# More load buffers, later kept loads and one re-cut row visit in a two-layer graph kernel

## What is computed

```python
def _L0_gnn_ref(X, adj, W, b):
    adj_hat = adj + eye
    d_inv_sqrt = 1.0 / sqrt(sum(adj_hat, axis=1))
    adj_norm = adj_hat * d_inv_sqrt[:, None] * d_inv_sqrt[None, :]
    return relu(adj_norm @ (X @ W) + b)

def _L1_gnn_ref(x, adj, weight, self_weight):
    support = x @ weight
    output = relu(support + adj @ support + x @ self_weight)
    return pair_norm(output)          # one mean per feature and one norm over all rows

x = _layernorm(x + _L0_gnn_ref(x, adj, L0_gnn_W, L0_gnn_b))
x = _layernorm(x + _L1_gnn_ref(x, adj, L1_gnn_weight, L1_gnn_self_weight))
```

## Time and profile before

| | before |
|---|---|
| median of 3 runs | 2022.59 us (2019.74 to 2023.22) |
| the profiled execution | 2021.88 us, its span 2020.1 us |
| stage 0 | 0 to 94.5 us |
| stages 1 to 7 | 94.5, 259.2, 406.4, 529.0, 630.3, 711.3, 772.0 (starts) |
| phase 2 | 852.1 to 1516.0 |
| phase 3 | 1516.0 to 1962.5 |
| tail | 1962.5 to 2020.1 |
| busy: PE, DVE, ACT | 1767.3, 1517.5, 1241.7 us |
| mean granted TensorE clock | 0.958 of full speed |

### The profile page before, as it was taken

The page is one execution under the profiler, slowest core; times in us unless marked ns, Lnnn a source line. Parts: engine busy times, 40 slices in busy tenths (PEclk is TensorE's granted clock), DMA queues, the critical chain, the costliest instruction groups (busy, mean ns, idle before and its releaser), DMA issues.

```text
span 2020.1 us, 21098 instructions
## 1 busy us (share of the span) xinstructions
PE 1767.3 (87%) x7682; PEld 1408.9 (70%) x7682; DVE 1517.5 (75%) x2165; ACT 1241.7 (61%) x1821; POOL 21.5 (1%) x34
## 2 busy tenths in 40 slices
PE   1199989889898986887999999999998999999992
PEld 0176777666776765665777887878886878778872
DVE  4586686686777785797775757557558999999996
ACT  3467667577666552563554445444446888888875
POOL 0000000000000000100000000000000000000001
PEclk7599999999999998899999999999999999999995
DMA  9999979889898772764445454554555999999972
GB/s 400 392 360 396 364 304 400 313 333 400 313 363 311 305 281 102 278 218 162 167 167 188 167 189 170 191 200 161 193 190 213 388 349 378 359 352 392 385 283 83
DMA packets 79144, 563.68 MB, mean 279 GB/s; under 512 B 8832, under 2 KB 8832, under 8 KB 11968
## 3 DMA queue, kind: packets, MB, share of 16 engines
q1 hardware_dynamic: 75456, 549.49, 71.0%
q0 software_dynamic: 3584, 12.85, 2.0%
HBM read 558.10 MB, written 4.19 MB: 278 GB/s over the span
## 4 chain that ended last, share of the span: by engine, by line
PE 50%; DVE 24%; DMA 15%; ACT 7%; issue 3%; SPq 0%; POOL 0%; ACTq 0%; DVEq 0%
PE acc L882 15%; PE acc L884 14%; PE acc L888 14%; DVE lo L600 13%; DMA raw<-in_adjN 9%; DMA raw<-in_adjT 5%; ACT hi L439 3%; ACT raw L445 3%; DVE s L620 2%; DVE rlo L598 2%; PE pC L864 1%; PE pD L864 1%; DVE s L606 1%; DMA o<-in_adjT 1%; PE pC L944 1%
## 5 line engine op out<-in xcount | busy, mean ns | idle before, releaser
L882 PE MATMUL acc<-hi,rhi 128*128 128x512 f32 x2048 | 834.6, 408 | 130.6 <-DVE lo L600 109.9
L439 ACT ACTIVATE hi<-raw 128x1024 fp32r<-128x1024 f32 x760 | 777.1, 1053 | 231.1 <-DMA raw<-in_adjT 115.7
L600 DVE TENSOR_TENSOR lo<-raw,hi 128x1024 fp32r<-128x1024 f32 x760 | 895.4, 1220 | 3.2 <-ACT hi L439 3.2
L884 PE MATMUL acc<-lo,rhi 128*128 128x512 f32 x2048 | 807.3, 394 | 0.0
L888 PE MATMUL acc<-hi,rlo 128*128 128x512 f32 x2048 | 638.5, 393 | 0.0
L882 PEld LDWEIGHTS acc<-hi,rhi 128*128 128x128 f32 x2048 | 389.3, 190 | 268.2 <-DVE lo L600 167.9
L888 PEld LDWEIGHTS acc<-hi,rlo 128*128 128x128 f32 x2048 | 388.1, 190 | 84.0
L884 PEld LDWEIGHTS acc<-lo,rhi 128*128 128x128 f32 x2048 | 390.3, 191 | 80.7 <-issue 5.0
L598 DVE TENSOR_TENSOR rlo<-zr,rhi 128x256 fp32r<-128x256 f32 x256 | 108.4, 423 | 350.7 <-ACT hi L439 350.3
L433 ACT ACTIVATE rhi<-zr 128x256 fp32r<-128x256 f32 x256 | 104.5, 408 | 263.3 <-PE acc L888 227.8
L445 ACT ACTIVATE raw<-raw 128x1024 f32<-128x1024 f32 x154 | 161.3, 1049 | 69.4 <-DMA raw<-in_adjN 69.2
(11 more groups left out here) (124 smaller groups left out, 784.5 us busy)
## 6 DMA issues: line engine op xcount, KB each, us to landing
raw<-in_adjT SPq DMA_DIRECT2D x380, 1024.0 KB, 6.1
raw<-in_adjN SPq DMA_DIRECT2D x112, 1024.0 KB, 7.7
o<-in_adjT SPq DMA_DIRECT2D x32, 1024.0 KB, 8.8
s<-in_xT POOLq DMA_DIRECT2D x8, 512.0 KB, 4.5
s<-in_x POOLq DMA_DIRECT2D x8, 512.0 KB, 11.2
out<-zr POOLq DMA_DIRECT2D x8, 512.0 KB, 4.6
w<-in_W POOLq DMA_DIRECT2D x2, 64.0 KB, 6.4
t<-in_Wself POOLq DMA_DIRECT2D x1, 64.0 KB, 6.4
```

The source lines that it names most:

```text
L439: S.activation(hi[n % DEEP][:, :], slice_of(chunk, j), ACT.Copy).then_inc(hi_ready, 1)
L600: V.tensor_sub(lo[n % DEEP][:, :], slice_of(chunk, j), hi[n % DEEP][:, :].bitcast(f32)).then_inc(slice_split, 1)
L882: T.matmul(banks[h][:, :], a, hi[n % DEEP][:, part], start=(opens and j == 0), stop=False, skip_group_check=True)
L884: T.matmul(banks[h][:, :], a, lo[n % DEEP][:, part], start=False, stop=False, skip_group_check=True)
```

## The change

**Buffers.** Loads of products and sums get, beside the four `raw`, up to five more places of 1 MiB in memory that is not in use then: `s34` and `s56` (blocks 3 to 6 of `s1`) in stages 0 to 7, and of `zr` blocks 6 and 7 to stage 5, 4 and 5 to stage 3, 2 and 3 to stage 1. This makes 9 buffers in stages 0 and 1, then 8, 7 and in stages 6 and 7 six. Phase 2 has four. In phase 3 the three places of `zr` are back: seven. A queue worked out beforehand, in order of the uses, gives each quarter its buffer; one semaphore per buffer tells of landings. POOL waits for the last use of `s34` and `s56` before it loads x, and DVE waits for the last use of the places in `zr` before it writes z there.

**Kept quarters** stand behind the first 8 entries of `sums` instead of the first 4 (or at its end, if it is shorter); in stage 7 they stand beside products 4 to 7 instead of 0 to 3.

**Phase 2.** The L1 visit of row 7 [7] goes; row 7's visit in phase 3 has column 7 as well. In its place row 3 [7] of two layers is visited, not final; row 3's later visit has [6, 5, 4], is final and marked `added`: its L1 part is added to `o1` by DVE (`add_dual`), behind `sum_row`, and not copied by ACT. Row 3's first visit is read by `add_visit_up` (L0) and `copy_dual` (L1). Loads and matmuls are as many as before.

The diff, cut to its core:

```diff
-        sums[Q:Q] = kept
+        if k == NB - 1:
+            sums = [None] * Q
+        at = min(2 * Q, len(sums))
+        sums[at:at] = kept
...
     add_visit(6, (L0,), 2, [7], final=True)
-    add_visit(7, (L1,), 2, [7])
+    add_visit(3, (L0, L1), 2, [7])
     add_visit(5, (L0, L1), 2, [7], final=True)
     add_visit(4, (L0, L1), 2, [7, 6], final=True)
-    for k in (3, 2, 1, 0):
+    add_visit(3, (L0, L1), 2, [6, 5, 4], final=True, added=True)
+    for k in (2, 1, 0):
         add_visit(k, (L0, L1), 2, list(range(NB - 1, k, -1)), final=True)
-    add_visit(7, (L1,), 3, [6, 5, 4, 3, 2, 1, 0], last=True)
+    add_visit(7, (L1,), 3, [7, 6, 5, 4, 3, 2, 1, 0], last=True)
...
-        if chunk.kind != "keep" and not chunk.cached:
-            chunk.ring = ring
-            ring += 1
+    BORROWED = {"s34": NB - 1, "s56": NB - 1, "z67": 5, "z45": 3, "z23": 1}
+    LATE = ("z67", "z45", "z23")
+    free_buffers = deque([(f"raw{r}", ()) for r in range(4)] + [(b, ()) for b in BORROWED])
+    for chunk in chunks:
+        if chunk.kind == "keep" or chunk.cached:
+            continue
+        phase = visits[chunk.visit].phase if chunk.kind == "mul" else 1
+        if phase == 3 and not late:
+            late = True
+            free_buffers.extend((b, ("split", chunk.base)) for b in LATE)
+        while phase < 3 and free_buffers[0][0] in BORROWED and (
+                phase == 2 or chunk.stage > BORROWED[free_buffers[0][0]]):
+            free_buffers.popleft()
+        chunk.buf, chunk.after = free_buffers.popleft()
+        loads[chunk.buf] += 1
+        chunk.load = loads[chunk.buf]
+        free_buffers.append((chunk.buf, chunk.freed))
+        if phase == 1:
+            phase1_last[chunk.buf] = chunk.freed
...
-                elif chunk.ring >= 0:
-                    if chunk.ring >= RAW:
-                        by, count = ring_chunks[chunk.ring - RAW].freed
+                elif chunk.buf:
+                    if chunk.after:
+                        by, count = chunk.after
                         sp.wait_ge(raw_free[by], count)
                     src = adjN if chunk.kind == "sum" else adjT
-                    sp.dma_start(raw[chunk.ring % RAW][:, :],
-                                 src[chunk.row, chunk.col, chunk.q]).then_inc(loaded[chunk.ring % RAW], 16)
+                    sp.dma_start(raw[chunk.buf], src[chunk.row, chunk.col, chunk.q]).then_inc(loaded[chunk.buf], 16)
...
             pool.wait_ge(sums_closed, NB)
+            for b in ("s34", "s56"):
+                by, count = phase1_last[b]
+                pool.wait_ge(raw_free[by], count)
...
-                if at == 0 and row in DUAL_ROWS:
-                    copy_dual(visits[mul_chunks[n - 1].visit])
...
                 split_hi(chunk)
+                v = ended(n, 0)
+                if v is not None and visits[v].layers == (L0, L1) and not visits[v].added:
+                    copy_dual(visits[v])
...
                 dk = d[:, k * BG:(k + 1) * BG]
+                for b, rows in (("z23", (2, 3)), ("z45", (4, 5)), ("z67", (6, 7))):
+                    if k in rows:
+                        by, count = phase1_last[b]
+                        dve.wait_ge(raw_free[by], count)
...
+            def add_dual(v):
+                dve.wait_ge(slice_multiplied, v.end)
+                dve.wait_ge(dual_read, max(w.out for w in visits if w.layers == (L0, L1) and w.row == v.row and not w.final))
+                for h in range(H):
+                    last = V.tensor_add(half(o1, v.row, h), half(o1, v.row, h), acc[v.sets[L1]][h][:, :])
+                last.then_inc(dual_added, 1)
...
                 if at == 0:
-                    sum_row(visits[mul_chunks[n - 1].visit])
+                    v = visits[mul_chunks[n - 1].visit]
+                    sum_row(v)
+                    if v.added:
+                        add_dual(v)
...
-                if v is not None and visits[v].layers == (L0,) and not visits[v].final:
+                if v is not None and L0 in visits[v].layers and not visits[v].final:
                     add_visit_up(visits[v])
```

More of the change, by code:

```diff
@@ L2 @@
 from concourse import mybir
+from collections import defaultdict, deque
 from contextlib import ExitStack
@@ L20 @@
     tail: int = -1
-    ring: int = -1
+    buf: str = ""
+    load: int = -1
+    after: tuple = ()
     freed: tuple = ()
@@ L38 @@
     last: bool = False
+    added: bool = False
     out: int = -1
@@ L104, in graph_kernel @@
             chunks.append(chunk)
-            if n < len(sums):
+            if n < len(sums) and sums[n]:
                 chunks.append(sums[n])
@@ L127, in graph_kernel @@
     add_visit(6, (L1,), 3, [7, 6, 5, 4, 3, 2, 1, 0], last=True)
-    DUAL_ROWS = [v.row for v in visits if v.layers == (L0, L1)]
+    DUAL_ROWS = [v.row for v in visits if v.layers == (L0, L1) and v.final]
     FINAL_ROWS = [v.row for v in visits if v.final]
@@ L153, in graph_kernel @@
             chunk.freed = ("dve", dve_sums)
[L154 to L157 removed]
+    BORROWED = {"s34": NB - 1, "s56": NB - 1, "z67": 5, "z45": 3, "z23": 1}
+    LATE = ("z67", "z45", "z23")
+    free_buffers = deque([(f"raw{r}", ()) for r in range(4)] + [(b, ()) for b in BORROWED])
+    loads = defaultdict(int)
+    phase1_last = {}
+    late = False
+    for chunk in chunks:
[14 more added lines that the diff above has]
+            phase1_last[chunk.buf] = chunk.freed
     stat_end = [0] * stats
@@ L185, in graph_kernel @@
             if L1 in v.layers:
-                dual_out += 1
-                free[v.sets[L1]] = ("dual", dual_out)
+                dual_out += not v.added
+                added_out += v.added
+                v.out = added_out if v.added else dual_out
+                free[v.sets[L1]] = ("added", v.out) if v.added else ("dual", v.out)
         else:
@@ L241, in graph_kernel @@
         o1 = sb("o1", [P, NB * BLK])
-        raw = [sb(f"raw{r}", [P, TILE]) for r in range(RAW)]
+        raw_own = [sb(f"raw{r}", [P, TILE]) for r in range(4)]
         hi = [sb(f"hi{r}", [P, BLK], f32r) for r in range(DEEP)]
@@ L268, in graph_kernel @@
         kept = o1
+        raw = {f"raw{r}": raw_own[r][:, :] for r in range(4)}
+        raw |= {"s34": s1[:, 3 * BLK:5 * BLK], "s56": s1[:, 5 * BLK:7 * BLK],
+                "z67": zr[:, 6 * BLK:8 * BLK], "z45": zr[:, 4 * BLK:6 * BLK], "z23": zr[:, 2 * BLK:4 * BLK]}
         ones = w1
@@ L283, in graph_kernel @@
         sums = [pC, pD]
-        loaded = [sem(f"loaded{r}") for r in range(RAW)]
+        loaded = {b: sem(f"loaded_{b}") for b in raw}
         kept_in = [sem(f"kept_in{q}") for q in range(Q)]
@@ L355, in landed @@
                 return kept_in[chunk.q], 16 * (chunk.row + 1)
-            return loaded[chunk.ring % RAW], 16 * (chunk.ring // RAW + 1)
+            return loaded[chunk.buf], 16 * chunk.load
         def slice_of(chunk, j):
@@ L728, in add_self @@
                 if k in DUAL_ROWS:
-                    dve.wait_ge(dual_read, DUAL_ROWS.index(k) + 1)
+                    v = next(v for v in visits if v.row == k and v.layers == (L0, L1) and v.final)
+                    dve.wait_ge(dual_added if v.added else dual_read, v.out)
                     ins = V.tensor_add(half(o1, k, h), half(o1, k, h), pD[:, :])
```

12 lines of the change are left out of this document (6 added, 6 removed).

## The result

The changed kernel takes 1944.34 us (median of 4 runs, 1943.18 to 1949.46) against 2022.34 before (4 runs): ratio 0.9608, 95% interval 0.9587 to 0.9629. The forecast was 1943, its range 1921 to 1970. Beside each other once more, with 9 runs of before: 0.9606 (0.9586 to 0.9626). The profiled execution took 1943.18, its span is 1941.4, 78.7 us shorter.

A forecast was written before the change was run, and what follows sets the result against it. Loads were taken to bound phase 1's mixed blocks and a round trip of kept loads stage 7, PE phases 2 and 3; span 2020.1 - 66 - 18 + 11 - 6 = 1941, time 1943, range 1921 to 1970.

The forecast's parts named there:

- Item 1: Phase 1's 15 blocks whose steps also bring row-sum quarters (mixed) fall to PE's 18.1 us: -41.7, 2 charged for DMA tie.
- Enough, barely: Stage 2's mixed blocks eat 4.4 quarters loaded ahead, of 8 buffers less about 2 in use or in flight.
- rival B: Stages 1 and 2: sustained load rate only 373 GB/s, DMA share 1.00 throughout; 1960 us, chance 0.13.
- Item 2: Stages 1 to 5, block beside kept quarters: coming behind a mixed block hides some DVE excess, up to 9 us, 4 taken.
- Item 3: Stage 7: cached block 11.6 instead of 39.8 us, next block 2.9 longer, last block 2 shorter; sum -27.
- Item 4: Phase 1: new waits imperfectly covered, one in three mixed blocks a microsecond late; 5 us taken off the gain.
- Item 5: Phase 2, two-layer block behind row 6: pair of visits 57.7 us (+3.7), PE gap about 7, row 3 later -21.8; -18.
- rival C: Phase 2: the two-layer pair costs its upper bound and the clock falls in the gap; +8, 1951 us, chance 0.10.
- Item 6: Phase 3: four L1 steps more, +11; seven buffers remove part of the DMA waits, -6.
- A: Phase 1: mixed blocks stop at 19.5 us, short of PE's floor; 21 us less gain, 1964 us, chance 0.22.
- D: SP's one in-order queue: waits at its head hold back free buffers, no further reach ahead; 1982 us, chance 0.06.
- E: Queued loads share the engines and land bunched, 12.4 us at each of six stage starts; 2057 us, chance 0.03.

The follow-up runs named there:

- half loads: Second half of stage 1 to 6 row-sum loads left out: from the changed kernel 1945.0 us, ratio 0.9617; from the kernel before 2010.3 us, ratio 0.994.

## Right and wrong, point by point

**Item 1, mixed blocks: mechanism right, size near.** PE's floor came as computed (18.2 with PE full). The tie with the DMA in stage 1, and with it the 2 us charged, came from 398 GB/s as the DMA's rate. That was the rate of loads issued late. With nine buffers it moves 420 all through stage 1, 2.49 us a quarter, so 52 quarters land by 85 + 130 = 215, seven us before the engines want the last. "Enough, barely" was too dark a view of eight buffers, and the step that failed is the reading of the earlier trace rows: share 1.00 beside 398 GB/s was not the DMA's best, as stage 0's 420 in the same group said. The experiment with half loads says the same from the other side. One sign named for rival B, a DMA share of 1.00 all through stage 1, came without B (1.01): at 420 GB/s it means a DMA that works ahead. (The 131 and 113 us of engines for stages 2 and 3 are 2 us under the item's own blocks, 133.1 and 115.0; measured 132.2 and 113.8, and nothing hangs on it.)

**Item 2, kept block: right in kind.** 4 us taken, at most 9; measured 6.8 by the pair of kernels with and without the move.

**Item 3, stage 7: right.** 11.6, 19.9 and 19.7 make 51.2; the forecast's 11.6, 19.9 and 21.3 make 52.8. The last block holds 90 matmuls instead of 108: most of PE's arrears went, 3.6 us where I took 2.

**Item 4, cover: mis-sized.** 5 us were set aside for mixed blocks that come late. Few do; the waits for adjT that are left are 10.3 us on ACT. Of the 8 us by which phase 1 beat the forecast, items 1 and 4 make 3.6 (38.3 by the buffers alone against 34.7), item 2 makes 2.8 and item 3 makes 1.9.

**Item 5, the two-layer block: the step that failed.** The pair of visits takes 26.3 + 36.9 = 63.2 us where I had 57.7; row 3's later visit, 72.2, is as said (93.9 - 21.8 = 72.1). The gap was 8.8 and not 7: I had row 6's normalisation hide under row 3's last step and gave 12 for the case that it doesn't. It doesn't: the split ahead of it can start only when PE is done with row 3's third step, and takes ACT and DVE as long as PE's last step takes, so that the normalisation begins at 859.57, 0.2 us before PE stops. The gap is then 4.6 for it, 3.0 for the second split and 1.3 for the add; ACT's part, which I had counted, runs beside it. The rest of the miss is the clock. PE runs at half rate for 4.9 us behind this gap and for 3.6 behind the one of 3.83 at the opening of row 3's visit, 4.2 us lost together, and the window's granted clock is 0.86. That was rival C, and it came: +5.5 of its +8. That this part nets to nothing I did not see; it is what the two kernels with and without it show.

**Item 6: right in kind.** +10.9 for four steps. -3.5 for -6: I took what reached PE of all waits for `lo`, 7.6, as caused by loads; 5.4 of those are there without any wait for a load.

**Rivals.** A is out: mixed blocks reach PE's floor. B is out by the half loads. C came in part. D is out: SP's queue does run ahead, even with the kept loads early (38.3 us less in stages 1 to 5). E is out: the page after gives a median of 15.7 us from issue to landing for row-sum loads, six quarters' time, but the 264 loads that SP issues in the first 780 us land in the order of issue without an exception, half of them 2.49 us or less behind the one ahead, and ACT's waits for adjT are 10.3 us in all. Of the Trainium skill's 358 GB/s ("DMA: Bandwidth & Descriptors", Specifications) this trace shows 420 over 150 us on end, so that figure doesn't bind one core by itself here.

## What to carry to other kernels

A wait for loads beside a full-looking DMA is no proof that bytes are the bound: look at the bytes a second in the same window against the best window of the trace, and at whether the DMA idles elsewhere in the same stage. If it does, try depth first: here two more buffers gave four fifths of what five could. Where the trace has the landings, see whether the loads that land late were issued late. A wait on an accumulator bank costs what stands ahead of the freeing instruction in its engine's order, and here the half clock behind the gap besides: moving one add by one step was worth 10.6 us, the re-cut of the visits around it nothing that could be measured.

## What the chip showed that I had not expected

The loads' rate rose with the depth of their queue, where the share read nearly the same: four mixed blocks at 398 GB/s and 1.00 with four buffers, at 382 and 0.99 in another execution of the same order of loads, and all of stage 1 at 420 and 1.01 with nine. Row-sum loads of half the size moved 298 to 318 GB/s at a share of 0.85 to 0.89. The DMA share is thus a poor measure of how near the DMA is to its best rate. A load issued 4 us or more before the one ahead of it landed lost under 0.2 us in the second window of the earlier trace rows; one issued later lost up to 1.6 us.

In row 3's first visit and behind it the half clock lasted 4.9 us behind a gap of 8.8 us and 3.6 us behind one of 3.8, and did not come behind one of 1.2. That each gap here cost half of such a stretch besides its own length was not in the forecast's sum, though the window before showed a clock of 0.90.
